# A GRU step's update factor by scalar_tensor_tensor, table rows set singly, and two banks by turns for the expert blocks' first products

## The reference

```python
def cell(h, x):
    gi = x @ W_ih + b_ih
    gh = h @ W_hh + b_hh
    r = sigmoid(i_r + h_r)
    z = sigmoid(i_z + h_z)
    n = tanh(i_n + r * h_n)
    h_new = (1.0 - z) * n + z * h
...
probs = softmax(x @ w_gate)                # 8 experts, the best 2, weights normed to 1
act = silu_and_mul(x @ w_gate_up[e])       # 512 -> 2 * 256
eo = act @ w_down[e]                       # 256 -> 512
shared = silu_and_mul(x @ w_sh_gate_up) @ w_sh_down
out = x_in + routed + shared
```

## Time and profile before

| | us |
|---|---|
| median of three runs (lowest, highest) | 1206.61 (1204.44, 1210.73) |
| the profiled execution | 1212.29 |
| its span | 1210.5 |
| TensorE busy | 1036.3 (86%) |
| VectorE busy | 868.3 (72%) |
| ScalarE busy | 575.3 (48%) |
| GpSimd busy | 204.8 (17%) |

### The profile page before, as it was taken

The page is one execution under the profiler, slowest core; times in us unless marked ns, Lnnn a source line. Parts: engine busy times, 40 slices in busy tenths (PEclk is TensorE's granted clock), DMA queues, the critical chain, the costliest instruction groups (busy, mean ns, idle before and its releaser), DMA issues.

```text
span 1210.5 us, 35908 instructions
## 1 busy us (share of the span) xinstructions
PE 1036.3 (86%) x13452; PEld 624.6 (52%) x13452; DVE 868.3 (72%) x4089; ACT 575.3 (48%) x1877; POOL 204.8 (17%) x213
## 2 busy tenths in 40 slices
PE   2789888889999898999899989998998898888884
PEld 2556555556665454555455545554555454555452
DVE  5898999868889888677867786778787778721111
ACT  4755555645555543444344534443444444434442
POOL 0200011120111212111211121112020112233332
PEclk9899999999999999999999999999999999989998
DMA  8933454382774653633351244134341144488793
GB/s 307 391 146 97 141 191 169 106 214 74 261 271 164 195 158 71 227 80 63 115 175 28 54 118 166 35 54 175 123 131 47 28 141 133 137 275 273 183 290 45
DMA packets 66909, 183.13 MB, mean 151 GB/s; under 512 B 7737, under 2 KB 40288, under 8 KB 59168
## 3 DMA queue, kind: packets, MB, share of 16 engines
q1 hardware_dynamic: 45632, 107.74, 25.3%
q0 software_dynamic: 21104, 73.11, 22.8%
HBM read 137.01 MB, written 52.87 MB: 157 GB/s over the span
## 4 chain that ended last, share of the span: by engine, by line
PE 51%; DVE 27%; ACT 8%; issue 8%; DMA 4%; POOL 0%; POOLq 0%; SPq 0%; DVEq 0%; ACTq 0%
PE psG L711 17%; PE psG L717 14%; PE psU L774 6%; DVE arena L1040 5%; DVE arena L1038 5%; PE psS L818 5%; ACT arena L1418 3%; DVE arena L1062 3%; DVE arena L1048 3%; DVE arena L1050 3%; DVE arena L1058 3%; ACT arena L1422 3%; PE psD L786 3%; PE psO L839 2%; DVE arena L1042 2%
## 5 line engine op out<-in xcount | busy, mean ns | idle before, releaser
L711 PE MATMUL psG<-arena 128*32 128x384 f16 x4096 | 213.8, 329 | 86.2 <-DVE arena L1062 76.5
L1418 ACT ACTIVATE arena<-arena 128x32 f32<-128x32 f32 x256 | 58.7, 229 | 341.7 <-DVE arena L1042 341.6
L717 PE MATMUL psG<-arena 128*32 128x384 f16 x4096 | 212.0, 326 | 4.0 <-issue 3.9
L774 PE MATMUL psU<-arena 128*128 128x256 f16 (+1 forms) x1920 | 203.4, 252 | 0.2 <-DVE arena L934 0.2
L1038 DVE STREAM_TRANSPOSE arena<-psG 128x128 f32<-128x128 f32 x256 | 81.1, 317 | 147.7 <-PE psG L717 141.3
L774 PEld LDWEIGHTS psU<-arena 128*128 128x128 f16 x1920 | 157.4, 98 | 48.8 <-issue 13.5
L711 PEld LDWEIGHTS psG<-arena 128*32 128x32 f16 x4096 | 86.2, 96 | 185.7 <-DVE arena L1062 147.8
L1615 POOL DMA_INDIRECT y<-arena x55 | 87.3, 1588 | 402.9 <-DVE arena L1040 318.5
L717 PEld LDWEIGHTS psG<-arena 128*32 128x32 f16 x4096 | 110.1, 97 | 61.4 <-issue 4.8
L818 PE MATMUL psS<-arena 128*128 128x512 f16 x468 | 116.7, 380 | 13.4 <-DVE arena L1262 11.2
L1040 DVE STREAM_TRANSPOSE arena<-psG 128x256 f32<-128x256 f32 x256 | 104.2, 407 | 0.0
(11 more groups left out here) (162 smaller groups left out, 1609.6 us busy)
## 6 DMA issues: line engine op xcount, KB each, us to landing
arena<-expert_weights SPq DMA_DIRECT2D x39, 1536.0 KB, 16.1
arena<-wgu POOLq DMA_DIRECT2D x32, 512.0 KB, 5.5
expert_weights<-arena POOLq DMA_DIRECT2D x9, 1536.0 KB, 6.9
gi_scratch<-arena SPq DMA_DIRECT2D x84, 128.0 KB, 1.9
arena<-gi_scratch SPq DMA_DIRECT2D x14, 768.0 KB, 5.7
arena<-wd POOLq DMA_DIRECT2D x16, 512.0 KB, 5.6
arena<-x SPq DMA_DIRECT2D x8, 512.0 KB, 3.9
hidden_rows<-arena SPq DMA_DIRECT2D x16, 256.0 KB
```

What stands on the lines that cost most here:

```text
L711: e.matmul(psG[32 * j:32 * j + 32, 0:384], prev[:, c, 2:6].rearrange("p q n -> p (q n)"), whv[c][1][:, :, :, 32 * j:32 * j + 32], start=(c ...
L717: r = e.matmul(psG[32 * j:32 * j + 32, 0:384], prev[:, c, 0:4].rearrange("p q n -> p (q n)"), whv[c][0][:, :, :, 32 * j:32 * j + 32], star ...
L774: r = e.matmul(psU[u % 2][:, 256 * gu:256 * gu + width], half(W_GS + ex * 4 + c, pw)[:, o:o + 128], hh[:, 1 - ph, c, first:first + width], ...
L1418: e.activation(Ur, Ur, ACT.Tanh, scale=reg_tr).then_inc(th_r, 1)
```

## The change

`step(t)` computes the same zc by a scalar_tensor_tensor: the column is no longer the second scalar but a third operand, broadcast over 32 columns. `hid_init` and `y_init` hand their pieces over with the rows in another order, so that a row is a run of its own. From block KS + 1 on, the first products of every other block go to psG, which the recurrence has used until then; `up(k)` waits there for the emptying of block k - 2, and once for the last transposes of the recurrence.

```diff
--- before.py
+++ after.py
@@ -375,6 +375,10 @@
         psLG, psRK, psCT = psT[:, 0:16], psT[:, 0:16], psT[:, 16:24]
         psT16 = psT[:, 0:512].bitcast(F16)
 
+        def up_bank(k):
+
+            return psG if k > KS and (k - KS) % 2 else psS
+
         def gates_bank(n):
             return gi_ps[n] if n < 6 else gi_ps[n - 6] if n < 12 else (psS, psO)[n % 2]
 
@@ -811,11 +815,13 @@
                         e.wait_ge(ld_xw[(k - KS) % 6], 16 * ((k - KS) // 6 + 1))
                     else:
                         e.wait_ge(ld_w[dynamic(k) % 4], 16 * (dynamic(k) // 4 + 1))
-                    need(e, e_up, k)
+                    need(e, e_up, k if k < KS else k - 1)
                     if k == 0:
                         e.wait_ge(gi_ev_a, 12 * NBLK - 6)
+                    if k == KS + 1:
+                        e.wait_ge(tr_zn, T)
                 for j, (ph, pw) in enumerate(PROD):
-                    r = e.matmul(psS[:, 0:512], hT[k % 2][:, ph, c], ew_half(k, c, pw),
+                    r = e.matmul(up_bank(k)[:, 0:512], hT[k % 2][:, ph, c], ew_half(k, c, pw),
                                  start=(c == 0 and j == 0), stop=(c == KC - 1 and j == 2))
                 if c == KC - 1:
                     r.then_inc(e_mm, 1)
@@ -1050,7 +1056,8 @@
                 e.scalar_tensor_tensor(out=c3(qq), in0=c3(qq), scalar=0.5, in1=gt[:, 8:12, :],
                                        op0=ALU.mult, op1=ALU.add).then_inc(g_w, 1)
                 e.wait_ge(th_z, t + 1)
-                e.tensor_scalar(zc, Uz, -1.0, col(C_NH), ALU.add, ALU.mult).then_inc(g_zc, 1)
+                e.scalar_tensor_tensor(out=zc, in0=Uz, scalar=-1.0, in1=col(C_NH).broadcast_to([P, 32]), op0=ALU.add,
+                                       op1=ALU.mult).then_inc(g_zc, 1)
                 need(e, g_H, t)
                 e.scalar_tensor_tensor(out=zh, in0=Uz, scalar=1.0, in1=Hs, op0=ALU.add, op1=ALU.mult).then_inc(g_zh, 1)
                 e.wait_ge(th_n, t + 1)
@@ -1259,7 +1266,7 @@
             def e_up_(k):
                 x_ = Xe[k % 2]
                 e.wait_ge(e_gate, k + 1)
-                e.scalar_tensor_tensor(out=x_, in0=x_, scalar=col(C_UP[1]), in1=psS[:, 256:512],
+                e.scalar_tensor_tensor(out=x_, in0=x_, scalar=col(C_UP[1]), in1=up_bank(k)[:, 256:512],
                                        op0=ALU.mult, op1=ALU.mult).then_inc(e_up, 1)
 
             def e_low(k):
@@ -1494,7 +1501,7 @@
                 need(e, e_lo, k - 1)
                 if k == 0:
                     read_scale(1)
-                e.activation(Xe[k % 2], psS[:, 0:256], ACT.Silu, scale=reg_tg[1]).then_inc(e_gate, 1)
+                e.activation(Xe[k % 2], up_bank(k)[:, 0:256], ACT.Silu, scale=reg_tg[1]).then_inc(e_gate, 1)
 
             def e_high(k):
                 e.wait_ge(e_up, k + 1)
@@ -1587,15 +1594,18 @@
             def rows_init():
                 e.dma_start(row_d[:, :], rowinit).then_inc(st_rows, 16)
 
+            def by_row(a):
+                return a.rearrange("(a b) w -> b a w", b=16)
+
             def hid_init(b):
                 need(e, st_hid[b % 2], 16 * (b // 2))
                 last = 256 * b + 256 if b < NBLK - 1 else NTOK + DUMP
-                e.dma_start(hid_d[256 * b:last, :], hpad[256 * b:last, :]).then_inc(st_hid[b % 2], 16)
+                e.dma_start(by_row(hid_d[256 * b:last, :]), by_row(hpad[256 * b:last, :])).then_inc(st_hid[b % 2], 16)
 
             def y_init(b):
                 need(e, st_y[b % 2], 16 * (b // 2))
                 last = 256 * b + 256 if b < NBLK - 1 else NTOK + DUMP
-                e.dma_start(y[256 * b:last, :], xt[256 * b:last, :]).then_inc(st_y[b % 2], 16)
+                e.dma_start(by_row(y[256 * b:last, :]), by_row(xt[256 * b:last, :])).then_inc(st_y[b % 2], 16)
 
             def file(t, g, j):
                 in_step(t)
```

## The result

The changed kernel takes 1195.03 us, median of 4 runs (1192.02 to 1198.25), against 1206.79 (1204.44 to 1210.73, 4 runs) for the kernel before: ratio 0.9894, interval 0.9874 to 0.9914. The forecast was 1195.5. The profiled execution took 1195.19 us, its span 1193.4; the one before took 1212.29 and 1210.5.

What follows compares the result with a forecast made beforehand. VectorE's and ScalarE's chain was taken to decide each recurrence step. Profiled: 1212.3 - 8.2 (factor) - 1.9 (banks) - 3.9 (rows) = 1198.3; median: 1206.6 - 8.2 - 1.9 - 1.0 = 1195.5 us, range 1189.5 to 1203.5.

Steps and rivals of the forecast that it cites:

- held as well: Recurrence, factor L1053: the case that GpSimd's indirect DMA stretches the new form like the old, so the factor gains nothing.
- Rival (a): Recurrence, factor L1053: GpSimd holds the new form as the old one; median 1203.7 us, chance 0.10.
- which wipes out what TensorE gained before: Behind the recurrence: ScalarE waits for an addition's landing at 1129.17, so TensorE's earlier gain from two banks is lost.
- 1.9 us of slack: Last additions into y: one lands near 1191.4, the next starts at 1193.36, released by ScalarE; this gap caps the banks' gain.
- become the bound: Expert blocks: eight later blocks are worth 3.8 us, more than 1.9, so additions into y limit the gain to 1.9.
- Rival (b): Behind the recurrence: additions do not bind, so two banks give 6.2 us; median 1191.2 us, chance 0.14.
- I read it as code arriving late behind large pieces in the DMA engines: TensorE's 3.93 us stop inside L717 at 257.67: setting table rows singly gains 3.9 us profiled, 1.0 in the median.
- rival (e): Table rows: row pieces hold back weight loads that ScalarE awaits; slower, 1217.1 us with eight pieces, chance 0.05.
- smaller pieces would let the code through: DMA engines near the stop at 257.67: changing queue between packets, they would pass code sooner, and the 3.9 us would go.
- (c): TensorE's stop near 257 us was in the timed runs too and goes; median 1192.6 us, chance 0.12.
- (d): TensorE's stop near 257 us comes up elsewhere as instruction positions shift; median 1200.4 us, chance 0.09.
- Nine tenths of the span: Opening claim that the 256 steps of the recurrence take nine tenths of the span.

Runs made afterwards that it cites:

- the part alone: Kernel before with only the factor as scalar_tensor_tensor: 1206.78 us, ratio 0.9923; under Part 2, with only the two banks by turns: 1210.88 us, ratio 0.9970.
- the repeated run: The changed kernel unedited, run again beside the kernel before on another group's chip: 1201.84 us, ratio 0.9913.
- short ones: Additions into y behind the recurrence take 16 of 128 rows, on the kernel before plus new factor: one bank 1190.37 us, two banks 1186.14 us.

## Why the prediction was right

**Part 1: right, in mechanism and size.** 8.2 us were forecast, 8.7 lie in the stretched steps, 9.4 (6.8 to 11.8) came with the part alone. All 256 are at 0.19. The choice of 0.19 over "held as well" rested on L1058 inside GpSimd's time. L1062, the term with the old state, has the form of the new factor and now stands 57 times 0.55 us or more behind the start of an indirect DMA, inside it, and is never over 0.19; so its 0.43 in the earlier trace rows came from the L1053 before it, as taken. The new factor itself never starts later than 0.51 behind in the changed kernel's first profile; in the repeated run it does once, 1.03 behind (step 139), and in four other kernels it starts 0.54 behind where the old form is held: 0.18 or 0.19 each time. So it is free, and has not only won a race, as far as five places tell. Rival (a) is out.

The Trainium skill, page "SBUF — State Buffer", section "SBUF: two separate sides", lets a VectorE instruction with two SBUF inputs collide with a GpSimd one that reads SBUF. If GpSimd reads SBUF while it issues an indirect DMA, which no row shows, L1062 would by that have been stretched like the old factor; it was not in any of 57 places. Its other half, a lock by the two-port mode, agrees with 41 stretched factors and is not contradicted by the one at 928.99.

**Part 2: the mechanism right, the slack too small.** The period fell by the 0.46 us that was forecast as 0.48, and L1274 is what is late. 1.9 us were forecast; 3.5 lie between the two profiles, 3.6 (between 1.1 and 6.1) came with the part alone. Cut the stretch at the evacuation that waits for the landing, 1129.17 before and 1114.28 after. From the last step to there it is 81.9 and 80.7 us. But over all profiles with whole additions it is 81.6 to 83.7 with one bank (five) and 80.7 to 87.9 with two (seven): no gain shows, and these 1.2 us are scatter. So "which wipes out what TensorE gained before" held. From there to the span's end it is 81.3 and 79.1, and over all profiles 81.3 to 82.4 with one bank and 79.1 to 79.8 with two: 2.7 less on average. The term that was mis-sized is the "1.9 us of slack", taken from one profile: between the third last addition and the one before it lie 6.96 us there, but 5.9 to 7.4 over the one-bank profiles, and 5.0 to 6.0 with two banks, where a landing takes 4.6 to 4.8.

That the additions "become the bound" is true of some profiles only. In the changed kernel's first the third last one, at 1176.38, still waits for ScalarE, 1.2 us after the landing before it. So something else kept the eight later blocks from giving their 3.7 us. What the forecast left out is the clock behind the landing: 6.8 us at 1.2 GHz here and none before; 0 or 3.4 us in the five one-bank profiles, 3.4 to 10.2 in the seven with two banks, whose TensorE comes earlier to the landing and idles 3.3 to 9.7 us there, against 2.6 to 3.7. How much of the 3.7 it took, no run separates. Rival (b), 6.2, fails with whole additions; with short ones, and no such stretch of slow clock, 5.2 come.

**Part 3: wrong.** The step "I read it as code arriving late behind large pieces in the DMA engines" failed in its last words. The large pieces are gone, code by its packet still arrives late, and the stop is 3.69 us instead of 3.93. What makes it long is open. The price also left out the slower clock around the stop's end, 3.4 us at 1.2 GHz in both profiles. The packets are of 4 KB, and there are 1,920 more of them, not 4,350. The price of the edit was bounded rightly: 0.60 us an issue is far under 3.2, and rival (e) did not come. The Trainium skill, page "DMA: Bandwidth & Descriptors", section "Queues, rings and completion order", has an engine change queue between packets. The prediction drew from it that smaller pieces would let the code through; the rule may stand, and no run shows whether the packets of the profile are those that it means, but the 3.9 us did not come with 4 KB in place of 32 and 48.

**The sum.** Profiled, 1198.3 was forecast and 1195.2 came. Of the 14.0 us, 8.7 came of 8.2, 3.5 of 1.9 (1.2 of them scatter), 0.2 of 3.9. Beside them came 2.4 from late signals that are gone, which the experiments put down to the chip, 1.0 ahead of step 0 and some 1.3 spread over the recurrence; neither was followed up. For the median the forecast is only 0.5 us off, and that is luck: it counted 1.0 for a stop that stayed, and too little for the banks. Counting the stop at only a part for the timed runs was the right caution for a wrong reason; rivals (c) and (d) both supposed that it would move, and it stayed in every profile. The opening's "Nine tenths of the span" is 82% (994.9 of 1210.5 us); nothing in the sum rests on it.

No version that computes the whole result beats the changed kernel by more than the runs can tell. The changed kernel without its rows and with later weight loads are within 0.2% of it.

## What to carry to other kernels

Where one engine's short instruction is the last link of every step, look in the timeline for the steps in which it is longer, and at what another engine does beside them; a neighbour that keeps its time there shows which form to use. Behind the first limit of a stage look for the next two: the next late operand made 0.48 us a block out of 0.90, and a chain of ordered transfers let about half of 6.2 us through. Look at the granted clock behind every longer idle time of TensorE: a wait of 4.9 us was followed by 6.8 us at half speed, one of 2.6 us by none. Take a slack from several profiles, since one is a draw (5.9 to 7.4 us here). Read a stop's cause in the trace before giving its removal a price: that a transfer was issued near it did not make it the cause.

## What was not expected of the hardware

- TENSOR_SCALAR on 128x32 f32 took 0.24 us with a column of SBUF as its scalar and 0.18 with numbers, which also all but ended the stretching (1 of 256 against 41).
- On one chip the step's last signal from TensorE came 0.1 to 0.6 us late beside back-to-back indirect DMAs in 14 to 23 steps, in each of four kernels; on two others, in each of eight kernels, in none or one (step 53, behind the stop, left out).
- An indirect addition of 16 rows still occupies GpSimd for 1.33 us against 1.58 with 128, and lands 2.8 to 7.8 us after its issue.
- SCALAR_TENSOR_TENSOR with the column broadcast as an operand was not held in any of 256 steps of eight profiles, where TENSOR_SCALAR with the same column was in 40 to 43.
